# Three edits to a written schedule: weight splits parted from their transposes, the ternary tail spread over the second attention, products of the shared expert put between transposes

## The chip, the core and the metric

The kernel runs on one core of a Trainium2 chip. PE (TensorE) multiplies and transposes, DVE (VectorE), ACT (ScalarE) and POOL (GpSimd) work on rows, SP (SyncE) issues most transfers. The metric is the device time of one execution in microseconds.

## The reference, cut to what matters

Sixteen sequences of 128 rows and 512 columns go through four residual steps, each on a layernormed x:

```python
x = x + tanh(g_xattn[0]) * L0_xattn(layernorm(x), ctx, mask, norm_w, wq, wk, wv, wo, wg)   # 16 heads, gated
x = x + tanh(g_ffn[0])   * L0_ffn(layernorm(x), weight, bias)    # rows quantised to 8 bits, weights to -1, 0, 1
x = x + tanh(g_xattn[1]) * L1_xattn(layernorm(x), ctx, ctx)      # sigmoid(Q'K), 512 x 512 scores
x = x + tanh(g_ffn[1])   * L1_ffn(layernorm(x), ...)             # 16 experts of 352, 4 a token, 2 shared ones
```

In the last step, sigmoid scores over 16 experts pick two of four groups and then four experts for each token; the shared expert (704 hidden columns, in two halves of 352) sees every token.

## The kernel before, in words

Every product of float32 operands is made of three: an operand is split into a high half (a copy rounded by ACT) and a low half (operand less high half, a subtraction on DVE or POOL), and `mm3` multiplies high by high, high by low and low by high. So whatever goes into a product is first transposed by PE into a PSUM bank, copied by ACT, subtracted by DVE.

The first three steps are one block. A list of words, `plan` (line 222 on), is the order of work. Each engine walks the whole plan and does its own part of each word, in order; semaphores with counts derived from the plan hold the engines together. Tiles of 128 rows are numbered 0 to 15; a number in a word is relative to a group of four tiles. The words that matter here:

- `W.k`: weight k is transposed in four tiles (PE) into a ring of four banks, with high halves on ACT and low halves on DVE. The ring (`RING`) is the two score banks, O and REC; a tile waits until the low half of the tile three before it is done.
- `sx` statistics of a tile of x (DVE); `xa`/`ra`, `xb`/`rb`, `xd`/`rd`: the row scales, small sums on DVE with a power on POOL after `ra` and after `rb`; `nm` normalises a tile (DVE); `xT`, `cT` transpose x or the context; `q.0.1`, `k.0.1` are projections of two tiles; `Sa`, `Sb` scores, `sm` softmax, `pT`, `pv`, `bc`, `rc`, `on`, `oT`, `oP` the rest of the heads. `Sa.0` writes the ring's banks and waits until all twenty tiles of weights are split (line 594 on).
- `st`, `ra`, `rb`, `rd`, `u`, `uT`, `fm`, `sf`: the ternary step of a tile: statistics, scales, quantisation on DVE (six instructions), transposes, the product, the sum into x on POOL, statistics for the next step. POOL also adds the bias row at `uT`.
- `an`, `qh`, `ks`: for the second attention, normalisation and high half of q on ACT; `ks` is a copy, a subtraction and the low half of q on POOL. `aS.b.n` are scores of tile b, quarter n, into a bank of the ring; `ag` their sigmoid (twice on ACT, low half on DVE), `aT` transposes the context, `ap` and `aO` the products with it, `aO` also the sum into x and its statistics on DVE. `sw` loads the first half of the shared expert. `ta`, `tb`, `tc` are the row scales for the last step.

The second attention is a loop of 64 steps m (`MS`): step m issues `aS` for m + 3, `ag` for m + 2, then `ap` for m. The dictionary `between` gives the words of the ternary step that come ahead of step m; there, `u.-2` is tile 14, `u.-1` tile 15.

The second block is `routing_and_shared_expert`. Its matrix of normalised rows, XT, is made tile by tile: ACT normalises (`norm`, into one of four places), PE transposes into one of two banks, ACT copies the high half, DVE subtracts the low half, and tile t waits for the low half of tile t - 2. After tiles 5, 9 and 13 PE does the logits of a group of four tiles, a product of the shared expert (`hidden`: eight triples of matmuls, four into bank A for w1 and four into bank B for w3) and the logits by row. `gated` is the silu (ACT), the product (DVE) and its split; it stands on ACT and DVE behind tiles 7, 11 and 15. The shared expert's first half is split in four parts: high halves on ACT (`split_hi`, behind tiles 1, 4 and 5), low halves on POOL. POOL also takes the power for the row scales of the last four tiles, whose sums DVE makes in `row_scale`.

A third block goes through the tiles of the sixteen experts.

Of the kernel before, what the change touches and what calls it, by code (L numbers as in the profile page):

```python
# [18 lines left out]
GB = 4  # L19
# [92 lines left out]
def attention_and_ternary(nc, c, x, g_x, g_f, fw, fb, ctx_in, mask, norm_w, wq, wk, wv, wo, wg, sw1, sw2, sw3):  # L112

    X, identF = c["X"], c["identF"]
    with ExitStack() as st:
# [71 lines left out]
        def steps(text, g):  # L187

            out = []
            for word in text.split():  # L190
# [26 lines left out]
                elif kind in ("xa", "xb", "xd"):  # L217
# [5 lines left out]
        start = ("W.k cT.0 cT.1 W.q sx.0 sx.1 sx.2 sx.3 xa.0 k.0.0 k.0.1 W.v xb.0 k.0.2 k.0.3 xd.0 nm.0 nm.1 W.g xT.0 xT.1 "  # L223
                 "mk.0 mk.1 mk.2 mk.3 q.0.0 q.0.1 nm.2 nm.3 W.o q.0.2 q.0.3 ")
# [3 lines left out]
        for g in range(NG):  # L228
            d = during.get(g, ("",) * 10)
            if g == NG - 1:  # L230
# [20 lines left out]
            "oP.3 uT.0 u.1 aS.0.2 fm.0 uT.1 fm.1 ", NG - 1)  # L251
        between = {0: "sf.-4", 1: "st.-2", 2: "sf.-3", 3: "st.-1", 5: "ra.-1", 6: "rb.-1", 7: "rd.-1 u.-2", 9: "uT.-2", 10: "u.-1",
                   12: "fm.-2", 13: "uT.-1", 16: "fm.-1", 18: "sf.-2", 20: "sf.-1", 22: "ta.1", 24: "tb.1", 26: "tc.1", 28: "sw", 36: "ta.2", 40: "tb.2",
                   42: "tc.2", 52: "ta.3", 56: "tb.3", 58: "tc.3"}
# [78 lines left out]
        with nc.Block() as block:  # L333
# [128 lines left out]
            def _(pe):  # L462
# [55 lines left out]
                for s in plan:  # L518
                    kind, t = s[0], s[1]
                    if kind == "W":  # L520
# [116 lines left out]
            def _(act):  # L637
# [4 lines left out]
                for s in plan:  # L642
                    kind, t = s[0], s[1]
                    if kind == "W":
                        for kc in range(KC):
                            f = KC * ORDER.index(t) + kc
                            act.wait_ge(w_tr, f + 1)
                            act.activation(W[t][:, 0, kc, :], RING[f % len(RING)][:, :], ACT.Copy, scale=scale_of(t, kc))\
                                .then_inc(w_hi, 1)
# [85 lines left out]
            def _(dve):  # L735
# [95 lines left out]
                for s in plan:  # L831
                    kind, t = s[0], s[1]
                    if kind == "W":
                        for kc in range(KC):
                            f = KC * ORDER.index(t) + kc
                            dve.wait_ge(w_hi, f + 1)
                            dve.scalar_tensor_tensor(out=W[t][:, 1, kc, :], in0=RING[f % len(RING)][:, :], scalar=scale_of(t, kc),
                                                     in1=W[t][:, 0, kc, :].bitcast(F32), op0=ALU.mult,
                                                     op1=ALU.subtract).then_inc(w_lo, 1)
# [166 lines left out]
def routing_and_shared_expert(nc, c, m, gate_w, ebias, w1, w2, w3, sw1, sw2, sw3):  # L1006
# [4 lines left out]
    with ExitStack() as st:  # L1011
# [96 lines left out]
        FIRST_SPLIT_AT = (1, 4, 5)  # L1108
# [15 lines left out]
        with nc.Block() as block:  # L1124
# [37 lines left out]
            def _(pool):  # L1162
                for n in range(PARTS):
                    if n == 2:
                        row_power(pool, c, scales, slice(3 * GB, NB), powered)
                    raw, hi, lo = part(0, n)
                    pool.wait_ge(w_hi, n + 1)
                    pool.tensor_tensor(lo, raw, hi.bitcast(F32), ALU.subtract).then_inc(w_lo, 1)
# [50 lines left out]
            def _(pe):  # L1219
# [27 lines left out]
                def hidden(q):  # L1247
# [8 lines left out]
                    for W_, bk in ((W1[b], A[q % 2]), (W3[b], B[q % 2])):  # L1256
                        for k in range(KC):
                            x_ = mm3(pe, bk[0:IC[ch], :], lambda j: W_[:, j, k, cols],
                                     lambda j: XT[:, gr, j, k, :], k == 0, k == KC - 1)
                    x_.then_inc(ab_fill, 1)  # L1260
# [72 lines left out]
                for t in range(NB):  # L1333
# [8 lines left out]
                    if t % GB == 1 and t > GB:  # L1342
                        logit(t // GB - 1)
                        hidden(t // GB - 1)
# [94 lines left out]
            def _(dve):  # L1439
# [221 lines left out]
                def split_lo(n):  # L1661
                    raw, hi, lo = part(1, n)
                    dve.wait_ge(w_hi, PARTS + n + 1)
# [16 lines left out]
                for t in range(NB):  # L1680
# [6 lines left out]
                    if t == GB:  # L1687
# [4 lines left out]
                                      XT[:, t // GB, 0, :, t % GB * P:(t % GB + 1) * P].bitcast(F32), ALU.subtract).then_inc(t_lo, 1)  # L1692
                    if t % GB == GB - 1 and t > GB:
                        gated(t // GB - 1)
# [331 lines left out]
```

## Time and profile before

| what | value |
|---|---|
| three runs, median | 1298.67 us (1297.68 to 1304.92) |
| profiled execution | 1298.22 us |
| its span, first to last instruction | 1296.5 us |
| PE, DVE, ACT, POOL busy | 94%, 52%, 44%, 33% of the span |
| mean granted TensorE clock | 0.981 |

The busy shares are averages over stages with different limits, so the stages have to be read one by one. The granted clock is a share of full speed: 1.00 is 2.4 GHz, 0.50 is 1.2 GHz, and values between are means over a stretch that has both.

### The profile page before, as it was taken

The numbers are of one execution on the slowest core, as the hardware profiler recorded it, in microseconds if no ns is written. First come the engines' busy times: TensorE is split into PE (matmuls) and PEld (weight loads), VectorE is DVE, ScalarE is ACT, GpSimd is POOL, SyncE is SP. The second block draws the span as 40 slices with busy tenths as digits, with TensorE's granted clock in tenths as the row PEclk, the third lists the DMA queues.
The fourth block names the chain that finished last, engine by engine and source line by source line (L and its number), as shares of the span: only waits on it lengthen the run. The fifth ranks groups of instructions, "written<-read, shape, count | busy, mean of one in ns | idle before, by whom it ended". The sixth has DMA issues, their size and how long they took to land. (4 is left out here: it accounts for less than half of the span.)

```text
span 1296.5 us, 25673 instructions
## 1 busy us (share of the span) xinstructions
PE 1215.9 (94%) x7824; PEld 1026.1 (79%) x7836; DVE 668.9 (52%) x1410; ACT 575.7 (44%) x1384; POOL 430.9 (33%) x518
## 2 busy tenths in 40 slices
PE   6998999999999789988999998999999999999995
PEld 6877778788787567666777786889998989999995
DVE  6556545555545799843666644542233553424241
ACT  4555456356356668763121111543334553434342
POOL 1102211210213466340004761244434444343433
PEclk9999999999999889979999999999999999999998
DMA  9100000000000003022000221765446666645554
GB/s 334 36 17 20 18 1 20 18 1 18 17 18 1 26 26 108 8 107 100 1 1 1 91 108 59 249 165 90 76 76 148 176 150 153 146 81 135 86 140 73
DMA packets 54335, 100.36 MB, mean 77 GB/s; under 512 B 5094, under 2 KB 21990, under 8 KB 54262
## 3 DMA queue, kind: packets, MB, share of 16 engines
q0 software_dynamic: 15824, 37.76, 15.5%
q1 hardware_dynamic: 38438, 61.65, 14.7%
q8 instruction: 43, 0.70, 0.2%
q14 instruction: 30, 0.25, 0.1%
HBM read 72.91 MB, written 26.48 MB: 77 GB/s over the span
## 5 line engine op out<-in xcount | busy, mean ns | idle before, releaser
L1876 PE MATMUL t_H<-m_W,t_xT 128*128 128x352 f32 x1632 | 280.2, 327 | 6.4 <-DVE m_W L1954 4.9
L1876 PEld LDWEIGHTS t_H<-m_W,t_xT 128*128 128x128 f32 x1632 | 261.6, 188 | 9.6 <-DVE m_W L1954 7.5
L1844 POOL DMA_INDIRECT out_dram<-t_ys,t_sid x68 | 109.6, 1612 | 220.4 <-ACT t_ys L1905 107.3
L1921 ACT ACTIVATE t_sl<-t_H 128x352 f32<-128x352 f32 x68 | 31.6, 464 | 174.0 <-PE t_H L1876 174.0
L722 ACT ACTIVATE pr<-SC,neg 128x128 f32<-128x128 f32 x256 | 89.9, 377 | 38.2 <-DVE neg L927 38.2
L46 PE MATMUL t_Y<-m_W,t_hT 128*128 128x512 f32 (+1 forms) x207 | 87.4, 422 | 5.2 <-issue 3.1
L1999 DVE TENSOR_TENSOR t_hT<-t_TH,t_hT 128x384 fp32r<-128x384 f32 x68 | 37.8, 556 | 101.9 <-ACT t_hT L1942 100.8
L1905 ACT ACTIVATE t_ys<-t_Y,t_wcol 128x512 f32<-128x512 f32 x69 | 47.4, 687 | 93.7 <-PE t_Y L48 93.7
L1975 DVE TENSOR_TENSOR t_h<-t_H,t_sl 128x352 f32<-128x352 f32 x68 | 35.5, 523 | 102.5 <-ACT t_sl L1921 102.2
L48 PE MATMUL t_Y<-m_W,t_hT 128*128 128x512 f32 (+1 forms) x207 | 81.8, 395 | 0.0
L47 PE MATMUL t_Y<-m_W,t_hT 128*128 128x512 f32 (+1 forms) x207 | 81.5, 393 | 0.0
L451 POOL TENSOR_TENSOR X<-X,upd 128x512 f32<-128x512 f32 x16 | 20.6, 1287 | 139.5 <-DVE upd L908 139.4
L421 POOL TENSOR_TENSOR tmp<-tmp,nhalf 128x2 f32<-128x2 f32 (+2 forms) x22 | 19.6, 892 | 131.6 <-DVE tmp L753 113.0
L667 ACT ACTIVATE pT<-T 128x512 f32<-128x512 f32 x64 | 38.4, 602 | 53.9 <-PE T L488 53.8
L924 DVE TENSOR_REDUCE mx<-SC 128x4 f32<-128x512 f32 x64 | 43.9, 685 | 33.8 <-PE SC L609 33.8
L1197 POOL TENSOR_SCALAR m_W<-m_W,bst 128x128 fp32r<-128x128 f32 x64 | 49.5, 793 | 31.6 <-PE eL L1311 31.4
L853 DVE TENSOR_TENSOR Wq<-kT,Wq 128x512 fp32r<-128x512 f32 x64 | 53.3, 852 | 5.8 <-ACT Wq L713 5.5
L1387 ACT ACTIVATE ehT<-eh 128x512 fp32r<-128x512 f32 (+1 forms) x24 | 15.2, 632 | 91.9 <-DVE eh L1670 91.9
L722 ACT ACTIVATION_READ_ACCUMULATOR pr<-SC,neg 128x1 f32 x256 | 55.3, 216 | 0.0
L1835 POOL COPY t_sid<-m_vals 128x1 uint32 x68 | 49.7, 731 | 0.9 <-issue 0.9
L46 PEld LDWEIGHTS t_Y<-m_W,t_hT 128*128 128x128 f32 (+1 forms) x207 | 39.0, 188 | 13.8 <-issue 5.4
L1950 DVE TENSOR_TENSOR t_xT<-t_TX,t_xT 128x512 fp32r<-128x512 f32 x69 | 47.6, 690 | 3.2 <-ACT t_xT L1898 0.4
(474 smaller groups left out, 3225.6 us busy)
## 6 DMA issues: line engine op xcount, KB each, us to landing
m_raw<-in_L_ffn_w_dram SPq DMA_DIRECT2D x28, 704.0 KB, 5.2
m_raw<-in_L_ffn_w_dram SPq DMA_DIRECT2D x14, 512.0 KB, 6.5
rows_d<-before_w SPq DMA_DIRECT2D x17, 256.0 KB, 2.0
CT<-in_ctx_dram SPq DMA_DIRECT2D x8, 512.0 KB, 3.7
X<-in_x_dram SPq DMA_DIRECT2D x4, 1024.0 KB, 13.9
out_dram<-X SPq DMA_DIRECT2D x3, 1024.0 KB, 4.3
m_raw<-in_L_ffn_w_dram SPq DMA_DIRECT2D x14, 192.0 KB, 6.4
CT<-in_ctx_dram SPq DMA_DIRECT2D x8, 256.0 KB, 2.7
```

Of the source, the lines that this page charges most:

```text
L46: pe.matmul(out, lhs(0), rhs(0), start=first, stop=False)
L47: pe.matmul(out, lhs(0), rhs(1), start=False, stop=False)
L48: return pe.matmul(out, lhs(1), rhs(0), start=False, stop=last)
L722: i = act.activation(pr[:, t % 2, slot, :], SC[t % 2][:, slot * S:(slot + 1) * S], ACT.Exp, scale=SCALE0, bias=neg[:, t % 2, slot:slot + 1 ...
L853: dve.tensor_tensor(as_[:, n, 1, :], asg[:, n, :], as_[:, n, 0, :].bitcast(F32), ALU.subtract).then_inc(as_lo, 1)
L924: dve.tensor_reduce(mx[:, t % 2, :], bk, AX.X, ALU.max).then_inc(s_out, 1)
L1197: i = pool.tensor_scalar(tab_a[t % SLOTS][:, k, :], iP.bitcast(F32), place_p[:, t, k:k + 1], None, ALU.is_equal)
L1835: pool.tensor_copy(sid[:, b:b + 1], m["target"][:, bass.ds(n, 1)]).then_inc(zeroed, 1)
L1844: pool.indirect_dma_start(out=m["out_rows"][:, :], out_offset=bass.IndirectOffsetOnAxis(ap=sid[:, b:b + 1], axis=0), in_=ys[:, b, :], in_o ...
L1876: x_ = pe.matmul(bk[b % 2][:, 0:I], xT[:, b % 2, jx, k, :], W13[:, jw, k, j, :], start=k == 0 and jx == jw, stop=k == KC - 1 and jx == 1)
L1905: act.activation(ys[:, (b - 1) % UT, :], Y[(b - 1) % 2][:, :], ACT.Copy, scale=wcol[:, (b - 1) % UT:(b - 1) % UT + 1]).then_inc(y_evac, 1)
L1950: dve.tensor_tensor(xT[:, b % 2, 1, :, :], TX[:, :].rearrange("p (k t) -> p k t", k=KC), xT[:, b % 2, 0, :, :].bitcast(F32), ALU.subtract) ...
```

## The change

Three things are moved; nothing is computed otherwise.

1. At the beginning a weight's word `W` becomes two for q, v, g and o: `Wt.q`, the transposes on PE, and `Ws.q.0` to `Ws.q.3`, its high and low halves tile by tile on ACT and DVE. The statistics of x come ahead of the splits of q, xT ahead of those of v, and g and o are split between and behind the q products.
2. In the last group of the heads `aT.0` and `aS.0.2` come earlier, and `uT` and `fm` of the group's second tile go into the steps of the second attention. The words of `between` are set at wider distances, up to step 30 instead of 20 for the ternary step.
3. In the routing, `hidden` is done in two halves, w1 behind the transposes of the third tile of a group and w3 behind those of the fourth, and the low halves of the first half of the shared expert go from POOL to DVE, behind tiles 0, 1, 5 and 6.

```diff
-        start = ("W.k cT.0 cT.1 W.q sx.0 sx.1 sx.2 sx.3 xa.0 k.0.0 k.0.1 W.v xb.0 k.0.2 k.0.3 xd.0 nm.0 nm.1 W.g xT.0 xT.1 "
-                 "mk.0 mk.1 mk.2 mk.3 q.0.0 q.0.1 nm.2 nm.3 W.o q.0.2 q.0.3 ")
+        start = ("W.k cT.0 cT.1 Wt.q sx.0 sx.1 sx.2 sx.3 xa.0 Ws.q.0 Ws.q.1 k.0.0 Ws.q.2 k.0.1 xb.0 Ws.q.3 k.0.2 xd.0 nm.0 nm.1 "
+                 "k.0.3 Wt.v xT.0 xT.1 Ws.v.0 Ws.v.1 Ws.v.2 Ws.v.3 q.0.0 Wt.g q.0.1 mk.0 mk.1 mk.2 mk.3 nm.2 nm.3 "
+                 "Ws.g.0 Ws.g.1 Ws.g.2 Ws.g.3 q.0.2 Wt.o q.0.3 Ws.o.0 Ws.o.1 Ws.o.2 Ws.o.3 ")
...
-            "oP.2 rb.0 pv.6 pT.14 rc.3 aS.0.0 pT.15 rd.0 bc.3 aT.0 pv.7 on.3 oT.3 u.0 aS.0.1 ag.0.0 aT.1 ag.0.1 "
-            "oP.3 uT.0 u.1 aS.0.2 fm.0 uT.1 fm.1 ", NG - 1)
-        between = {0: "sf.-4", 1: "st.-2", 2: "sf.-3", 3: "st.-1", 5: "ra.-1", 6: "rb.-1", 7: "rd.-1 u.-2", 9: "uT.-2", 10: "u.-1",
-                   12: "fm.-2", 13: "uT.-1", 16: "fm.-1", 18: "sf.-2", 20: "sf.-1", 22: "ta.1", 24: "tb.1", 26: "tc.1", 28: "sw", 36: "ta.2", 40: "tb.2",
-                   42: "tc.2", 52: "ta.3", 56: "tb.3", 58: "tc.3"}
+            "oP.2 rb.0 pv.6 pT.14 rc.3 aS.0.0 pT.15 aT.0 rd.0 bc.3 pv.7 on.3 oT.3 u.0 aS.0.1 ag.0.0 aT.1 aS.0.2 ag.0.1 "
+            "oP.3 uT.0 u.1 fm.0 ", NG - 1)
+        between = {2: "uT.-3", 3: "sf.-4", 4: "fm.-3 st.-2", 6: "st.-1", 8: "ra.-1 sf.-3", 10: "rb.-1", 12: "rd.-1 u.-2", 17: "uT.-2",
+                   18: "u.-1", 20: "fm.-2", 23: "uT.-1", 25: "sf.-2", 26: "fm.-1", 28: "sw", 30: "sf.-1", 32: "ta.1", 34: "tb.1", 36: "tc.1",
+                   44: "ta.2", 48: "tb.2", 50: "tc.2", 52: "ta.3", 56: "tb.3", 58: "tc.3"}
...
-                    if kind == "W":
-                        for kc in range(KC):
+                    if kind in ("W", "Ws"):
+                        for kc in s[2:] or range(KC):
...
-        FIRST_SPLIT_AT = (1, 4, 5)
+        FIRST_SPLIT_AT, FIRST_LOW_AT = (1, 4, 5), (0, 1, 5, 6)
...
-                for n in range(PARTS):
-                    if n == 2:
-                        row_power(pool, c, scales, slice(3 * GB, NB), powered)
-                    raw, hi, lo = part(0, n)
-                    pool.wait_ge(w_hi, n + 1)
-                    pool.tensor_tensor(lo, raw, hi.bitcast(F32), ALU.subtract).then_inc(w_lo, 1)
+                row_power(pool, c, scales, slice(3 * GB, NB), powered)
...
-                    for W_, bk in ((W1[b], A[q % 2]), (W3[b], B[q % 2])):
+                    for W_, bk in [((W1[b], A[q % 2]), (W3[b], B[q % 2]))[n] for n in halves]:
...
-                    x_.then_inc(ab_fill, 1)
+                    if 1 in halves:
+                        x_.then_inc(ab_fill, 1)
...
                     if t % GB == 1 and t > GB:
                         logit(t // GB - 1)
-                        hidden(t // GB - 1)
+                    if t % GB == 2 and t > GB:
+                        hidden(t // GB - 1, (0,))
+                    if t % GB == 3 and t > GB:
+                        hidden(t // GB - 1, (1,))
                         logit_rows(t // GB - 1)
...
+                    if t in FIRST_LOW_AT:
+                        split_lo(FIRST_LOW_AT.index(t), 0)
```

## Rows read from the trace of the kernel before

**Rows 1.** The page, the line of busy engines.

```profile
PE 1215.9 (94%) x7824; PEld 1026.1 (79%) x7836; DVE 668.9 (52%) x1410; ACT 575.7 (44%) x1384; POOL 430.9 (33%) x518
```

**Rows 2.** Windows by stage: length, engines busy, clock, DMA share, GB/s.

```profile
0.00:39.24 39.24, 27.45 (x195) 26.44 (x197) 22.43 (x50) 18.45 (x35) 3.79 (x15) 0.96 0.80 285
39.24:421.00 381.76, 365.92 (x3269) 299.03 (x3279) 208.41 (x529) 198.45 (x729) 73.64 (x64) 1.00 0.06 15
421.00:549.00 128.00, 114.61 (x539) 86.75 (x539) 110.43 (x188) 95.64 (x181) 70.73 (x58) 0.95 0.14 42
549.00:609.15 60.15, 49.28 (x230) 35.35 (x230) 21.69 (x38) 29.90 (x46) 13.06 (x15) 0.86 0.31 111
609.15:807.55 198.40, 191.75 (x862) 149.63 (x862) 118.62 (x262) 34.10 (x52) 66.23 (x90) 0.99 0.12 41
807.55:1296.50 488.95, 466.93 (x2733) 428.91 (x2733) 187.28 (x344) 199.17 (x342) 203.48 (x277) 0.99 0.58 129
```

**Rows 3.** Timeline of PE: start, us, instruction, count, idle before it.

```profile
29.48 0.55 PE L46 MATMUL M<-xT,Wq 128*128 128x256 f32 x1 [3.20 <-DVE xT L872]
...
33.91 0.38 PE L474 MATMUL SC<-identF,pr 128*128 128x128 f32 x2
...
35.58 0.37 PE L46 MATMUL M<-xT,Wq 128*128 128x256 f32 x1
...
38.40 0.28 PE L48 MATMUL M<-xT,Wq 128*128 128x256 f32 x1
39.24 0.39 PE L601 MATMUL SC<-mrow,onesB 1*128 1x512 bf16 x2 [0.56 <-ACT qT L689]
```

**Rows 4.** Timeline of DVE at the start.

```profile
16.64 2.46 DVE L879 BATCH_NORM_STATS2 bst<-X 128x6 f32<-128x512 f32 x4
...
35.27 1.41 DVE L837 SCALAR_TENSOR_TENSOR Wo<-SC,hg,Wo 128x512 fp32r<-128x512 f32 x2 [4.48 <-ACT Wo L648]
...
37.26 0.74 DVE L837 SCALAR_TENSOR_TENSOR Wo<-REC,hg,Wo 128x512 fp32r<-128x512 f32 x1
```

**Rows 5.** Windows in four stretches, for the granted clock.

```profile
30.00:31.00 1.00, 1.00 (x7) 1.00 (x6) 0.79 (x2) 0.00 (x0) 0.00 (x0) 0.50 1.07 395
...
438.00:440.00 2.00, 2.00 (x7) 1.35 (x5) 1.06 (x2) 0.46 (x1) 0.66 (x2) 0.50 0.00 0
...
459.00:461.00 2.00, 2.00 (x6) 1.61 (x5) 2.00 (x4) 1.91 (x4) 0.24 (x1) 0.50 0.01 4
...
600.00:605.00 5.00, 5.00 (x17) 3.28 (x16) 0.69 (x1) 2.16 (x3) 0.00 (x0) 0.71 0.07 21
```

**Rows 6.** Who PE waited for, 421 to 549 us: total, times, longest.

```profile
PE T L488 <- DVE fu L803: 6.0, 2, 3.8
PE M L46 <- DVE oT L941: 1.6, 1, 1.6
PE SC L46 <- POOL Wk L444: 1.4, 2, 0.8
PE REC L631 <- DVE rec L933: 1.0, 1, 1.0
PE M L500 <- ACT fuT L672: 0.9, 1, 0.9
```

**Rows 7.** POOL's groups from 421 to 549 us: count, busy us, mean ns.

```profile
L444 POOL TENSOR_TENSOR Wk<-xn,Wk 128x512 fp32r<-128x512 f32 x14 | 20.2, 1441 | 31.1 <-ACT Wk L705 31.1
```

**Rows 8.** Who PE waited for, 549 to 609 us.

```profile
PE eY L1338 <- DVE XT L1691: 6.8, 6, 2.9
...
PE eL L1236 <- DVE XT L1691: 1.6, 1, 1.6
```

**Rows 9.** Timelines of DVE and of POOL at the beginning of the routing.

```profile
552.29 3.16 DVE L91 TENSOR_TENSOR mean<-bst 128x4 f32<-128x4 f32 x1
...
552.27 3.16 POOL L1168 TENSOR_TENSOR m_W<-shared_raw,m_W 128x1408 fp32r<-128x1408 f32 x1 [11.18 <-ACT m_W L1373]
```

**Rows 10.** Line 1664, the second half's low halves on DVE: ns min/median/max.

```profile
L1664 DVE TENSOR_TENSOR eW<-m_raw,eW x4: 683/1416/1618, 660.7 to 717.7; 128x1408 fp32r<-128x1408 f32 x2, 128x1024 fp32r<-128x1024 f32 x1, 96x512 fp32r<-96x512 f32 x1
```

More of the change, by code:

```diff
@@ L519, in _ @@
                     kind, t = s[0], s[1]
-                    if kind == "W":
+                    if kind in ("W", "Wt"):
                         weight(t)
@@ L643, in _ @@
                     kind, t = s[0], s[1]
-                    if kind == "W":
-                        for kc in range(KC):
+                    if kind in ("W", "Ws"):
+                        for kc in s[2:] or range(KC):
                             f = KC * ORDER.index(t) + kc
@@ L832, in _ @@
                     kind, t = s[0], s[1]
-                    if kind == "W":
-                        for kc in range(KC):
+                    if kind in ("W", "Ws"):
+                        for kc in s[2:] or range(KC):
                             f = KC * ORDER.index(t) + kc
@@ L1245, in logit_rows, with hidden @@
                     i.then_inc(logits, 1)
-                def hidden(q):
+                def hidden(q, halves=(0, 1)):
                     u, ch = q // 3, q % 3
@@ L1659, in tile_rows, with split_lo @@
                         .then_inc(meta_ok, 1)
-                def split_lo(n):
-                    raw, hi, lo = part(1, n)
-                    dve.wait_ge(w_hi, PARTS + n + 1)
+                def split_lo(n, b=1):
+                    raw, hi, lo = part(b, n)
+                    dve.wait_ge(w_hi, PARTS * b + n + 1)
                     dve.tensor_tensor(lo, raw, hi.bitcast(F32), ALU.subtract).then_inc(w_lo, 1)
```

## The prediction

> **What bounds the kernel now.** I read the page first: PE is busy for 94% of the span [rows 1], so a change can only pay where PE waits or where its clock is low. The windows by stage [rows 2] show where that is. From 39.24 to 421 us, and from 609 us on, PE is busy for some 96% of the time at a granted clock of 0.99 to 1.00; those stages are chains of products, and a shift ahead of them is carried to the end. The three stages that the change touches are the loose ones: the start (27.45 busy of 39.24 us), the end of the heads with the second attention (114.61 of 128.00 us, clock 0.95), and the routing (49.28 of 60.15 us, clock 0.86). Then I read, stage by stage, who PE waited for [rows 3, 6, 8], and the queues of DVE, ACT and POOL in order of time. ACT, DVE and POOL work through the same written plan as PE, in order, so moving a word in the plan moves it past everything queued on each of them.
>
> **Part one, the start.** What it removes: DVE's low halves of Wv and Wg stood between the statistics of x and the low half of xT, and the first q product waited 3.20 us for that [rows 3, 4]. From the first statistics (16.64) to q.0.0 (29.48) it took 12.84 us. Four low halves take 2.73 us (35.27 to 38.00, [rows 4]). Eight of them leave this stretch and the four of Wq enter it: 2.7 less. The two POOL powers between are then covered by less DVE work; I charge 0.9 as an estimate, which leaves 1.8. The statistics may also begin up to 2.7 earlier, as Wq's low halves no longer precede them, if x has landed. No row shows when it landed, so the gain lies between 1.8 and 4.5; I take the middle, 3.1.
>
> What it adds: the transposes are parted from the splits. Wt.g comes to stand between q.0.0 and q.0.1, while W.g filled a time in which PE had to wait for x anyway: 1.7 more (four tiles from 33.91 to 35.58, [rows 3]). On ACT, Ws.g now stands behind the eviction of q.0.1, and Wt.o needs the four banks that Ws.g frees. The chain from first transpose to last low half of a weight took 4.1 us (33.91 to 38.00, [rows 3, 4]); without the first tile's transposes (0.4) and with an eviction ahead (0.56, [rows 3]) it is 4.25. Wt.o thus ends some 4.8 after q.0.1, and q.0.3 1.55 later: 6.35, where it was 4.77 (33.91 to 38.68): 1.6 more. Last, Sa.0 waits for all twenty low halves, and Ws.o now stands behind q.0.3 on ACT: Sa.0 follows q.0.3 by 4.25 where it followed by 0.56: 3.7 more. So 7.0 lost against 3.1 won: 3.9 later.
>
> The gap before Sa.0 also touches the clock. After the 3.20 us gap the clock was at 0.50, 1.2 GHz [rows 5], and q.0.0 with q.0.1 took 4.43 us where q.0.2 with q.0.3 took 3.10 [rows 3]: 1.3 lost. The new gap is longer, so I add 1.3 (bounds 0 and 1.3), and leave the old fall before q.0.0 in place, since PE is mostly idle there in the new order too; without it 1.3 would come back. **The start: 5.2 us later** (bounds 1.2 and 6.5). The Trainium skill has the same reading (TensorE: Matmul & The Clock Gate, "What's actually happening"): the low clock is the resting state and activity lifts it, so an order that trades one gap for another keeps paying; the row at 30 us agrees.
>
> **Part two, the tail.** Before, the last heads ended with u.13, uT.13 and fm.13 in a row, and tile 14 followed within the first steps. PE waited 6.0 us for two quantisations, 1.6 for oT, 1.0 for rec, 0.9 for uT, and 1.4 for POOL's low half of q [rows 6]: 10.9. After the gaps the clock lay at 0.50 twice, some 6 us each [rows 5]; PE was busy for about 10.6 us of that, half of which is lost: 5.3. So 16.2 can be won. I worked the new order forward by the durations of the old one. aT.0 goes into the wait for rec (0.55 of it is left), aS.0.2 into that for oT (0.5 left). With aS.0.2 gone from its old place, fm.0 waits about 1.3 for ACT's uT. uT.13 finds its tile ready. What is late next: ap.1.0 waits 0.4 for DVE to empty aO.0's bank. POOL has fm.12's and uT.13's adds before ks.2, so aS.2.0 waits 1.1. At step 12, ks.4 stands on POOL behind the second power, which waits for DVE's rb; casts, subtraction and aq's low half (1.44 a row, [rows 7]) then end 1.8 to 2.7 after PE wants aS.4.0: 2.2. And u.15 on DVE holds back the eviction of aO.4: 1.7. Sum of the new waits 7.75. The clock fell behind the gaps of 3.20 and 3.8 us and not behind that of 1.6; a fall cost 2.7 here (half of 5.3), and for the gap of 2.2, between these rows, I take half of one, 1.3 (bounds 0 and 2.7). **The tail: 16.2 - 7.75 - 1.3 = 7.2 us earlier** (bounds 3 and 11, as POOL keeps pace with PE or not). The adds and statistics moved to steps 8 to 30 lie beside products; without that cover each add is 1.3.
>
> **Part three, the routing.** PE waited 6.8 us before transposes and 1.6 before the last logits for the low half of XT [rows 8]. With two banks and one pair of copies a tile, ACT and DVE pace four transposes in a row while the product of 5.6 us stands in one piece. Between transposes, each half covers a tile. In the steady part the waits were 1.06 and 0.56 in two groups and 1.57 at the end: 4.8, all of it covered. The stretch of the last logits ran at a clock of 0.71 after that wait [rows 5]: 29% of 5 us, 1.4, comes back. At the beginning DVE's first small sum took 3.16 us, begun 0.02 us after POOL's 3.16 us low half [rows 9]; its six sisters take 0.15 to 0.17. That block of 3.0 goes with POOL's work, but DVE now does two low halves of the 1408 columns, 1.4 to 1.6 each [rows 10], ahead of XT's third low half. Net 0.8 won. What queues behind the new waits: ACT's gated(q) now waits for a half product that PE issues after tile 7's transposes, and tile 8's copy stands behind it; by the rows it is ready just as PE comes to tile 10. **The routing: 7.0 us earlier** (bounds 3.5 and 8). The Trainium skill (SBUF - State Buffer, "Who interferes with whom") says that a DVE instruction with two SBUF inputs and a GpSimd instruction that reads SBUF exclude each other for the whole instruction. Rows 9 agree; by that rule the moved low halves still shut POOL out, but its one power there is 1.0 us, so the sum stays.
>
> **Sum.** The profiled execution took 1298.22 us (span 1296.5 and 1.7 around it), 0.45 below the median of 1298.67. 1298.2 + 5.2 - 7.2 - 7.0 = 1289.2.
>
> **Rivals.** First: the start gains what its gap promised. The 3.1 us at q.0.0 would be carried on, if Ws.o were done by the time of q.0.3; then 1298.2 - 3.1 - 7.2 - 7.0 = 1280.9. For it speaks that ACT was idle 5 us before q.0.0's eviction; against it that Ws.o stands behind q.0.3 in the plan. Second: the second attention takes its gain back. POOL, with 1.44 us for a low half [rows 7] and the adds spread over seven tiles, becomes the pace: the 7.2 are lost, 1296.4. The Trainium skill's rule of exclusion is the mechanism behind such a pace; rows 9 show one case. Third: ACT, waiting for half products, starves the transposes in the routing: half of part three is lost, 1292.6. Fourth, slower: the new waits on POOL, one in each tile, keep the clock at 1.2 GHz through steps 8 to 26 of the second attention. At that clock three products took 1.28 us where they otherwise take 0.69, so a tile of eight such triples and its transposes costs some 5.1 us more. 1.8 tiles eat the sum, from 3.1 tiles on the kernel is slower by more than 0.5%; all 4.5 tiles give 1312. Against it: after both falls the clock came back within 7 us though waits went on.
>
> **How the numbers follow.** The forecast has 0.57 (1284 to 1294), the first rival 0.10, the second 0.15, the third 0.14, the fourth 0.04. Under 0.5%, 6.5 us, a measurement of this kernel can't be told from no change; 1292.2 is the border. The forecast's own range lies four fifths under it (0.46), with the first rival and half of the third 0.63 faster; 0.33 the same; 0.04 slower. The range 1281 to 1297 holds the forecast and the second and third rivals, 0.86.
>
> **What would show it.** Right: q.0.0 begins near 26.4, but Sa.0 only near 43 to 44; a gap of some 4 us before Sa.0; no gap over 2.5 us between 421 and 475; aS.4.0 waits for POOL; DVE L91 takes 0.15; no wait for XT before tiles 8, 9, 12, 13. Wrong: Sa.0 at or before 39.24, a low clock through more than one tile after 450, or gaps before transposes in the routing.

## The result, and the profile after

The changed kernel takes 1295.38 us (median of 13 executions, 1291.82 to 1299.50); the kernel before took 1304.35 beside it (13 executions, 1297.68 to 1306.27). The ratio is 0.9942, with a 95% interval of 0.9927 to 0.9958: faster by 0.58% (0.42 to 0.73), where the prediction had set 0.5% as the least that can be told from no change. Of the 13 executions of the kernel before, five took 1297.68 to 1299.51 us and eight 1303.31 to 1306.27; the profiled one (1298.22), on which the forecast was built, is like the five. The changed kernel's profiled execution took 1294.01 us (span 1292.3), 4.2 less. The forecast was 1289.2, so the time is 6 us above it: outside the forecast's own 1284 to 1294, inside the wide range of 1281 to 1297. The forecast's three terms were +5.2 (start), -7.2 (tail) and -7.0 (routing); I read them off one by one.

The page's line of busy engines, for [rows 1], and the windows by stage, for [rows 2] (length, then busy time of PE, PEld, DVE, ACT, POOL, then clock, DMA share, GB/s):

```profile
PE 1212.3 (94%) x7823; PEld 1023.5 (79%) x7836; DVE 672.5 (52%) x1414; ACT 575.9 (45%) x1384; POOL 424.8 (33%) x514
```

```profile
0.00:40.82 40.82, 26.25 (x196) 24.32 (x198) 22.67 (x50) 17.80 (x35) 3.80 (x15) 0.98 0.77 274
40.82:425.84 385.02, 368.48 (x3269) 300.44 (x3279) 208.66 (x529) 198.80 (x729) 73.77 (x64) 0.99 0.05 15
425.84:552.05 126.21, 112.41 (x538) 85.20 (x539) 111.28 (x188) 95.85 (x181) 72.08 (x58) 0.97 0.14 43
552.05:603.80 51.75, 45.96 (x230) 34.03 (x230) 23.58 (x42) 30.03 (x46) 5.02 (x11) 0.90 0.37 130
603.80:801.68 197.88, 191.39 (x862) 149.50 (x862) 118.70 (x262) 34.13 (x52) 66.42 (x90) 0.99 0.12 41
801.68:1292.30 490.62, 467.85 (x2733) 430.00 (x2733) 187.56 (x344) 199.32 (x342) 203.75 (x277) 0.99 0.57 129
```

The busy shares are those of before, so as totals they say nothing. By stage: the beginning is 1.58 us longer, the heads 3.3 longer (with the same work), the second attention 1.8 shorter, the routing 8.4 shorter. In the second attention PE's idle time did not fall: 128.00 less 114.61 before, 126.21 less 112.41 after, which is 13.39 and 13.80 us. What it won there is 2.2 us of busy time, at a clock of 0.97 in place of 0.95. PE's timeline at the start answers [rows 3]; under it stand four windows, one at q.0.0 and three around Sa.0:

```profile
26.06 0.36 PE L46 MATMUL M<-xT,Wq 128*128 128x256 f32 x1 [1.65 <-DVE xT L873]
...
32.83 0.41 PE L475 MATMUL SC<-identF,pr 128*128 128x128 f32 x2 [0.51 <-DVE Wg L838]
...
40.82 0.61 PE L602 MATMUL SC<-mrow,onesB 1*128 1x512 bf16 x2 [3.97 <-issue]
```

```profile
26.00:28.00 2.00, 1.94 (x16) 1.97 (x17) 2.00 (x4) 1.27 (x4) 0.00 (x0) 1.00 1.05 386
...
38.00:40.00 2.00, 0.00 (x0) 0.00 (x0) 2.00 (x4) 1.58 (x3) 0.00 (x0) 0.80 0.00 0
...
42.00:44.00 2.00, 2.00 (x14) 1.47 (x12) 0.01 (x1) 0.60 (x1) 0.00 (x0) 0.50 0.00 0
...
46.00:48.00 2.00, 2.00 (x7) 1.52 (x6) 0.24 (x2) 2.00 (x13) 0.00 (x0) 0.50 0.05 12
```

q.0.0 begins 3.4 us earlier than before, and Sa.0 1.58 later: the gap ahead of Sa.0 is there as forecast (3.97 us), reached sooner than forecast. At q.0.0, behind a gap of 1.65 us, the clock is at 1.00, where it was at 0.50 before. But from the gap ahead of Sa.0 to 48 us the clock is at 0.50, with PE busy all the time from 42 us on. The transposes of cT.2 begin at 49.57; before, they began at 44.14: 5.43 late, of which 3.85 arose behind Sa.0.

PE's waits from the last heads to the end of the second attention answer [rows 6], those of the routing [rows 8], DVE's first small sum [rows 9]:

```profile
PE SC L46 <- POOL Wk L445: 5.4, 5, 2.2
PE M L46 <- DVE X L859: 2.7, 1, 2.7
PE M L46 <- issue: 2.1, 2, 1.1
PE M L501 <- DVE upd L909: 1.1, 1, 1.1
...
PE REC L632 <- DVE rec L934: 0.6, 1, 0.6
PE M L46 <- DVE oT L942: 0.5, 1, 0.5
```

```profile
PE eY L1335 <- DVE before_w L1676: 2.5, 1, 2.5
PE eY L1335 <- ACT before_w L1394: 1.7, 1, 1.7
PE eY L1335 <- DVE XT L1691: 1.7, 2, 1.0
```

```profile
555.34 0.15 DVE L91 TENSOR_TENSOR mean<-bst 128x4 f32<-128x4 f32 x1
```

The two waits of 6.0 us in all for a quantisation are gone, and so are 6.7 us of waits for XT. What PE waits for in the second attention is now above all POOL (5.4 us) and one sum of DVE's (2.7).

The table takes the same instructions in each trace: the time in the kernel before, and by how many us a kernel is later (+) or earlier (-). The four lower lines are the first four experiments.

| | Sa.0 | Sa.2 | aS.0.0 | routing's first transposes | experts' first transposes | PE's last |
|---|---|---|---|---|---|---|
| before, us | 39.24 | 58.06 | 419.72 | 551.43 | 807.55 | 1285.72 |
| changed | +1.58 | +5.44 | +4.84 | +3.05 | -5.87 | -4.11 |
| beginning alone | +2.29 | +5.37 | +5.27 | +4.93 | +8.99 | +9.43 |
| tail alone | +0.74 | +0.75 | +1.01 | -0.63 | +1.10 | +2.21 |
| routing alone | +1.95 | +1.96 | +1.15 | -0.30 | -9.01 | -5.90 |
| tail and routing | +0.94 | +0.96 | +0.36 | -1.37 | -10.00 | -6.99 |

In the changed kernel the beginning costs 4.8, the tail wins 1.8 (4.84 to 3.05), the routing 8.9, and 1.8 of that is given back among the experts, so that 7.2 are left at the end. The term that failed is the tail's.

### The profile page after: what moved, and what is told of

Same layout as the page of the kernel before. It is cut to its first block and busy times, and to the rows that moved or that the text cites. A ratio compares the mean times of both kernels' runs of the same rounds, so it can differ in the third digit from the quotient of the medians.

```text
span 1292.3 us, 25672 instructions
## 1 busy us (share of the span) xinstructions
PE 1212.3 (94%) x7823; PEld 1023.5 (79%) x7836; DVE 672.5 (52%) x1414; ACT 575.9 (45%) x1384; POOL 424.8 (33%) x514
## 5 line engine op out<-in xcount | busy, mean ns | idle before, releaser
L854 DVE TENSOR_TENSOR Wq<-kT,Wq 128x512 fp32r<-128x512 f32 x64 | 53.3, 855 | 5.4 <-ACT Wq L714 5.2
```

The costliest lines, as they stand in the source:

```text
L854: dve.tensor_tensor(as_[:, n, 1, :], asg[:, n, :], as_[:, n, 0, :].bitcast(F32), ALU.subtract).then_inc(as_lo, 1)
```

## The experiments

### One part at a time

The beginning alone:

```diff
 # kernel before, with
-start = ("W.k cT.0 cT.1 W.q sx.0 ...")
+start = ("W.k cT.0 cT.1 Wt.q sx.0 ... Ws.o.0 Ws.o.1 Ws.o.2 Ws.o.3 ")
```

> The kernel before with the new order of the beginning alone. By the offsets of the two traces the beginning costs about 4.8 us, whatever follows it: Sa.0 near 40.8 us with a gap of about 4 us ahead of it, clock 0.50 from there to about 48 us, routing and second attention as before, span 1301 to 1302. The rival, that the later stages absorb a late beginning (their first waits are for loads and other engines, which a shift leaves where they are), would give a span within 2 us of 1296.5.

1307.28 us (median of 10) beside 1301.81 for the kernel before; ratio 1.0033 (1.0011 to 1.0055). Sa.0 had the same 3.97 us ahead of it, and of the 5.3 us at aS.0.0 4.9 were left at the routing: next to nothing absorbs a late beginning. The 4 us more at the experts' first transposes arose in the routing, together with the delay that the next experiment shows.

The tail alone:

```diff
 # kernel before, with
-"... rd.0 bc.3 aT.0 pv.7 ...", between = {0: "sf.-4", ...}
+"... aT.0 rd.0 bc.3 pv.7 ...", between = {2: "uT.-3", ...}
```

> The kernel before with the new end of the heads and the new steps of the second attention alone. If what this edit brings is limited by its own queues (POOL's low half of q, DVE's sum into x ahead of tile 5), it gives about 1.8 us here too: span near 1294.7, with PE waiting 2 to 2.7 us ahead of aS.4.0 and of ap.5.0 again. The rival, that the edit is worth the 7.2 us of the sum and lost the rest only in company with the late beginning, gives a span near 1289.3 and neither of these waits.

1299.12 us (10 executions), ratio 0.9967 (0.9950 to 0.9984). From aS.0.0 to the routing it wins 1.64 (+1.01 to -0.63), with the same waits as in the changed kernel. So the tail's small gain is its own and no consequence of the late beginning. It is nearer 0.9 than 1.8: in the four profiled executions with the old tail and no other change to that stage it takes 130.26 to 131.71 us (mean 131.0, the profile of before being the longest), in five with the new tail 129.92 to 130.94 (mean 130.2).

The trace shows something else as well: this execution lost 2.9 us at the first logits, in code that is that of before. Timelines of POOL and of DVE there:

```profile
555.32 3.15 POOL L1168 TENSOR_TENSOR m_W<-shared_raw,m_W 128x1408 fp32r<-128x1408 f32 x1 [0.52 <-ACT m_W L1373]
```

```profile
555.47 3.03 DVE L97 TENSOR_SCALAR tmp<-tmp 128x4 f32<-128x4 f32 x1
```

A DVE instruction on 4 columns takes 3.03 us, begun 0.15 us after a subtraction of POOL, and ends with it; in the profile of before the same instruction took 0.17, just ahead of POOL's second subtraction. With the beginning alone it took 3.07. This is [rows 9] a second time, and here it is a matter of chance: the code is the same in all three kernels.

The routing alone:

```diff
 # kernel before, with
+FIRST_LOW_AT = (0, 1, 5, 6)     # POOL's low halves to DVE
-    hidden(t // GB - 1)
+    hidden(t // GB - 1, (0,)) at the third tile, (1,) at the fourth
```

> The kernel before with the routing's edit alone. If the halves of the product between the transposes are what takes the waits away, it gives about 7.2 us alone: span near 1289.3, waits for XT under 2 us, clock 1.00 from 565 to 610 us. The rival, that part of the gain came from the stage being reached at another time against its loads, gives a gain of 5 us or less.

1292.47 us (4 executions, 1291.96 to 1293.06), ratio 0.9912 (0.9880 to 0.9944). The stage wins 8.7 us, and its waits for XT are 1.7. At the end 5.6 of the 8.7 are left; the rest goes among the experts, whose stage I did not take apart.

Tail and routing, with the old beginning:

```diff
 # changed kernel, with
-start = ("W.k cT.0 cT.1 Wt.q ...")
+start = ("W.k cT.0 cT.1 W.q ...")
```

> The changed kernel with the old order of the beginning. If the three parts add up, it takes the gain of the tail and of the routing without the cost of the beginning: span near 1287.5 (9 us under before, 4.8 under the changed kernel). If the parts hang together, the sum of the other three runs does not give this one; a span of 1290 or more would say so.

1290.87 us (4 executions), ratio 0.9894 (0.9859 to 0.9928), span 1289.7. Faster than the changed kernel, as the sum says, though 2 us short of the span expected: it reaches Sa.0 0.9 later than before did (the three kernels of this group with the old beginning, 0.7 to 2.0), and gives back 3 us among the experts. Part of the late Sa.0 is the clock: behind the same gap of 3.20 us ahead of q.0.0 it stayed at 0.50 for 3.4 us in the profile of before, and for 6.8 us here and with the routing alone.

The low halves of the shared expert on DVE, with the product in one piece:

```diff
 # the routing alone, with
-    hidden(t // GB - 1, (0,)) at the third tile, (1,) at the fourth
+    hidden(t // GB - 1) at the second tile, as before
```

> The kernel before, with one half of the routing's edit: the low halves of the first half of the shared expert go to DVE, and the product stays in one piece. If what changes from one execution of the kernel before to the next is whether DVE's last small sum is caught behind POOL's second low half (0.17 us in the profiled one, 3.03 and 3.07 in two profiled runs that keep the old routing), both blocks of 3 us go: the first logits begin 1.3 us earlier than in the profile of before, the times lie within 2 us of each other, and their median is 1296 to 1298, 4 to 5 us under that of before. The rival, that the steady waits ahead of tiles 8, 9, 12 and 13 hold all of the gain, leaves times spread from 1298 to 1306 with the median of before. Both leave those four waits (1.06 and 0.56 us twice) in place.

1297.18 us, four executions within 1.4 us (1296.01 to 1297.36), beside 1303.40; ratio 0.9948 (0.9932 to 0.9965). DVE L91 took 0.14 and L97 0.17, and the first logits came 1.43 earlier against the stage's beginning. The waits for XT stayed (5.6 and 1.6). So this half takes away the chance delay, and the product's halves take away the steady waits: 8.7 less the 0.5 that this kernel wins in the stage against the profiled execution of before. Whether the delay is all that spreads the times of the kernel before is not shown: with it the stretch from the routing's first transposes to the experts' took 1.7 us (tail alone) and 4.1 us (beginning alone) longer than in the profile of before, while the 13 times of that kernel range over 8.6 us; and the changed kernel, in whose profile DVE's small sums are not delayed, still ranges over 7.7.

### The gap ahead of Sa.0

A product put into the gap:

```diff
-"... q.0.3 Ws.o.0 Ws.o.1 Ws.o.2 Ws.o.3 "     ... "sm.1 v.0 st.-2 ..." in group 0
+"... q.0.3 Ws.o.0 Ws.o.1 Ws.o.2 Ws.o.3 v.0 " ... "sm.1 st.-2 ..." in group 0
```

> The changed kernel, with the product v.0 of the first group taken from behind the first scores and put between q.0.3 and Sa.0, where PE waited 3.97 us for the last low half of Wo. It is 2.8 us of products, so the wait should shrink to 1.1 to 1.3 us. If the low clock from 40.8 to 48 us is what the gap ahead of it leaves behind, it goes too: the transposes of cT.2 then begin near 43 us (49.57 in the changed kernel), and the kernel is 6 to 6.7 us faster. The rival, that the clock falls because of how little PE did from 27 to 41 us altogether, gives the 2.8 us alone, with 0.50 still shown behind Sa.0. A third: the softmax of the first heads now has 2.8 us less beside it, and PE waits before pT.0 for what it won.

1291.96 us, ratio 0.9907 (0.9891 to 0.9924). PE's timeline:

```profile
41.00 0.39 PE L603 MATMUL SC<-mrow,onesB 1*128 1x512 bf16 x2 [1.19 <-issue]
...
42.99 0.66 PE L490 MATMUL T<-identF,CT 128*128 128x128 f32 x4
...
48.82 0.63 PE L490 MATMUL T<-identF,pr 128*128 128x128 f32 x4 [1.54 <-ACT xT L666]
```

```profile
38.00:41.00 3.00, 1.81 (x9) 1.17 (x7) 2.94 (x5) 1.76 (x4) 0.00 (x0) 1.00 0.00 0
41.00:44.00 3.00, 2.77 (x27) 2.14 (x28) 1.36 (x3) 0.60 (x1) 0.00 (x0) 1.00 0.00 0
44.00:48.00 4.00, 3.28 (x16) 2.42 (x15) 1.31 (x4) 3.39 (x18) 0.00 (x0) 1.00 0.02 6
```

The low clock is gone altogether and cT.2's transposes begin at 42.99 instead of 49.57: the fall followed the gap, and what PE did before 36 us is the same in both kernels. (The product also adds to PE's work from 27 to 41 us, so the second case is made unlikely and not ruled out.) At Sa.2 4.2 us are won, 4.4 against q.0.0; of the 2.4 that this lacks against cT.2's 6.6 the third case took 1.54, ahead of pT.0.

The high halves of Wo ahead of q.0.3:

```diff
-"... q.0.2 Wt.o q.0.3 Ws.o.0 Ws.o.1 Ws.o.2 Ws.o.3 "
+"... q.0.2 Wt.o Ws.o.0 Ws.o.1 Ws.o.2 Ws.o.3 q.0.3 "
```

> The changed kernel, with the high halves of Wo ahead of q.0.3 in the plan instead of behind it. If Sa.0 came late only because ACT and DVE took up Wo behind the eviction of q.0.3 (its transposes were done 1.5 us earlier), ACT makes the high halves from about 33.5 us on, the last low half is done near 37.5, Sa.0 begins near 37.7 (40.82 in the changed kernel), no low clock follows, and the kernel is some 7 us faster (3.1 of the wait, 3.85 of the clock). The rival, that DVE, which makes the masks and normalises two tiles in this stretch, sets the time of the low halves, leaves Sa.0 near 40; then no more than 1 us is won, and the clock falls as before.

1289.78 us (4 executions, 1288.68 to 1290.39), ratio 0.9900 (0.9872 to 0.9928): the lowest median of the study, if by 0.6 us only. DVE's last low half of Wo, and PE's Sa.0:

```profile
36.61 0.74 DVE L838 SCALAR_TENSOR_TENSOR Wo<-REC,hg,Wo 128x512 fp32r<-128x512 f32 x1
```

```profile
37.57 0.39 PE L602 MATMUL SC<-mrow,onesB 1*128 1x512 bf16 x2 [0.66 <-ACT qT L690]
```

Sa.0 is 3.25 us earlier than in the changed kernel, Sa.2 7.12, aS.0.0 6.26. One word in the wrong place turned a beginning that wins (1.4 us at aS.0.0) into one that loses.

### The tail

The product fm of tile 14 one step earlier:

```diff
-18: "u.-1", 20: "fm.-2", 23
+18: "u.-1", 19: "fm.-2", 23
```

> The changed kernel with one word moved by one step: the product fm of tile 14 from step 20 to step 19. Products of fm and sums of the second attention share two banks, and at step 20 the single fm between aO.4 and aO.5 gives ap.5.0 the bank that DVE has not yet emptied of aO.4, because u.15 stands before it on DVE. If that is why PE waited 2.67 us there, the wait goes (0 to 0.5 us comes up ahead of ap.4.0), the clock of 0.71 from 480 to 485 us goes too, and by the next steps some 3.5 us are won, of which the wait for POOL ahead of aS.8.0 (1.5) can take a part: 2 to 3.5 us faster in the end. The rival, that DVE as a whole is behind, moves the wait to the next product: within 0.7 us of the changed kernel.

1299.85 us, 4.5 us slower than the changed kernel by the trace at the routing. The wait at ap.5.0 went (2.67 to 0.42), and a wait of 4.64 for POOL came ahead of aS.6.0: POOL's sum now stands ahead of ks.6 and waits for DVE, which is at u.15. POOL's and PE's timelines:

```profile
479.10 1.65 POOL L460 TENSOR_TENSOR X<-X,upd 128x512 f32<-128x512 f32 x1 [6.29 <-DVE upd L916]
```

```profile
479.12 0.47 PE L46 MATMUL M<-Wq,Wv 128*128 128x512 f32 x1 [0.42 <-DVE upd L916]
484.69 0.79 PE L46 MATMUL SC<-Wk 128*128 128x512 f32 x1 [4.64 <-POOL Wk L445]
```

The second power behind ks.4:

```diff
-10: "rb.-1", 12: "rd.-1 u.-2", 17
+12: "rb.-1", 14: "rd.-1 u.-2", 17
```

> The changed kernel with the second small sum and power of tiles 14 and 15 behind ks.4 instead of ahead of it (rb from step 10 to 12, rd and u.14 from step 12 to 14). If POOL came late with the low half of q for tile 4 because it waited for DVE's sums ahead of the second power, the wait of 2.25 us ahead of aS.4.0 falls under 0.6 us and the 0.74 of clock behind it goes: 2 to 3.5 us faster at tile 5, if u.14, now 2 steps later, is not waited for. The rival, that POOL's own work paces this stretch (adds and low halves of 1.2 to 1.8 us each), leaves a wait of 1.5 us or more at aS.4.0 or moves it to aS.5.0.

1294.99 us, and 0.1 us of difference from the changed kernel between aS.0.0 and the routing. The wait at aS.4.0 went, as the first theory had it, and came back as 4.23 us for DVE, where u.14 now stood:

```profile
471.96 0.77 PE L46 MATMUL M<-Wq,Wv 128*128 128x512 f32 x1 [4.23 <-DVE Wv L866]
```

```profile
465.84 1.61 DVE L797 TENSOR_SCALAR fu<-X,mean,rstd 128x512 f32<-128x512 f32 x1
...
468.78 1.31 DVE L804 TENSOR_SCALAR fu<-fu,fsc 128x512 f32<-128x512 f32 x1
```

The words set wider still:

```diff
-between = {2: "uT.-3", 3: "sf.-4", 4: "fm.-3 st.-2", ... 12: "rd.-1 u.-2", ... 20: "fm.-2", ... 26: "fm.-1", ... 30: "sf.-1", ...
+between = {2: "uT.-3", 3: "sf.-4", 5: "fm.-3", ... 17: "u.-2", ... 24: "fm.-2", ... 30: "fm.-1", ... 33: "sf.-1", ...
```

> The changed kernel with the ternary words of the second attention spread further still: fm.13 at step 5, the sums and powers at 12 to 16, u.14 at 17, its product at 24, u.15 at 22, its product at 30, the last statistics at 33. If the stretch fails by its density (DVE and POOL each have too much in steps 4 to 26), the waits shrink and 2 to 4 us are won. If each lone fm costs a wait of its own through the bank that it takes, or the total of DVE's work sets the length, the result lies within 1 us of the changed kernel.

1294.57 us; 0.7 us won between aS.0.0 and the routing, no more than that stage differs between executions. The sums of waits are of the same size (4.6 for DVE ahead of two ap, 4.3 for POOL): density by itself is not the cause.

Less work on DVE, and less on POOL:

```diff
+w_ = slice(0, 8 if t >= NB - GB else D)
-dve.tensor_scalar(u[:, :], X[:, t, :], ...)      # and the reduction, and the rounding
+dve.tensor_scalar(u[:, w_], X[:, t, w_], ...)
```

> The changed kernel; the quantisation of tiles 12 to 15 is done on 8 of its 512 columns (the other columns are left out), which takes about 8 us from DVE between 425 and 490 us and nothing from POOL. DVE was busy for 63 of the 70 us from 430 to 500, more than PE. If DVE's load is what the spread words run into, the stage from aS.0.0 to the first transposes of the routing (129.9 us) gets 5 to 8 us shorter, and the waits for DVE's sum ahead of ap.5.0 (2.7) go, with part of those for POOL, whose inputs come from ACT and DVE. If POOL's queue is what paces it, the stage shortens by less than 1.5 us and the 5.1 us of waits for POOL stay.

```diff
+w_ = slice(0, 8 if t >= NB - GB else D)
-pool.tensor_tensor(X[:, t, :], X[:, t, :], brow[:, :], ALU.add)     # and the sum with upd
+pool.tensor_tensor(X[:, t, w_], X[:, t, w_], brow[:, w_], ALU.add)
```

> The changed kernel; POOL's sums into x of the ternary step (bias row and product) for tiles 12 to 15 are done on 8 of 512 columns (the rest is left out), which takes 8 additions of 1.3 to 1.7 us, some 10 us, from POOL and nothing from DVE's own work. If POOL's queue paces the stretch, its 5.1 us of waits go and the stage gets 5 us shorter or more. If DVE's load does, the waits ahead of ap.5.0 stay and the stage gains 2 us or less, out of instructions of DVE that no longer run beside an addition.

The first kernel quantises only 8 of the 512 columns of tiles 12 to 15, the second adds only 8 columns of the bias row and of the product; the rest is left out. The stage from aS.0.0 to the routing (129.92 us in the changed kernel) takes 127.79 with less on DVE and 124.25 with less on POOL: 2.1 and 5.7 won. (Their total times, 1317.98 and 1313.99, are not to be compared: other values of x lead to other routes, and the experts take 24 us longer.) From 430 to 500 us DVE was busy for 62.58 us with less on DVE, and for 63.19 in the changed kernel: hardly less, though 1.7 us of it are two instructions that only now fall into the stretch. The groups of DVE's instructions in that stretch, with less on DVE first, the changed kernel second:

```profile
L855 DVE TENSOR_TENSOR Wq<-kT,Wq 128x512 fp32r<-128x512 f32 x33 | 32.8, 1014 | 2.9 <-ACT Wq L714 2.9
...
L798 DVE TENSOR_SCALAR fu<-X,mean,rstd 128x8 f32<-128x8 f32 x4 | 3.0, 755 | 0.0
```

```profile
L854 DVE TENSOR_TENSOR Wq<-kT,Wq 128x512 fp32r<-128x512 f32 x32 | 29.4, 939 | 2.8 <-ACT Wq L714 2.7
...
L866 DVE TENSOR_TENSOR Wv<-T,Wv 128x512 fp32r<-128x512 f32 x7 | 4.8, 685 | 1.6 <-ACT Wv L660 1.6
...
L797 DVE TENSOR_SCALAR fu<-X,mean,rstd 128x512 f32<-128x512 f32 x4 | 4.1, 1013 | 0.0
```

And one of the four, with what POOL does beside it (timelines of DVE and POOL, less on DVE):

```profile
462.13 1.19 DVE L798 TENSOR_SCALAR fu<-X,mean,rstd 128x8 f32<-128x8 f32 x1
```

```profile
462.03 1.26 POOL L445 TENSOR_TENSOR Wk<-xn,Wk 128x512 fp32r<-128x512 f32 x1
```

With 8 columns instead of 512 the instruction takes 755 ns in place of 1013; in the heads, where POOL does little, all 512 columns take 541. Two of the four took 0.29 us; the other two took 1.19 and 1.26 us, begun beside an instruction of POOL's that was under way, and ended with it. The three groups of the quantisation together went from 10.5 to 5.5 us, not to the 2.5 expected, and the subtraction of two operands in SBUF (L854) got longer, 939 to 1014 ns. L866, which reads one operand from PSUM, takes 685 ns throughout. With less on POOL nothing was taken from DVE, and yet its subtraction took 824 ns in place of 939 (less on POOL):

```profile
L856 DVE TENSOR_TENSOR Wq<-kT,Wq 128x512 fp32r<-128x512 f32 x35 | 28.3, 824 | 4.7 <-ACT Wq L716 4.7
```

So part of DVE's time in this stretch is POOL's.

The casts of tiles 2 to 8 on ACT, on top of the early Wo; and the same with the wider words:

```diff
 # ACT, behind qh, for tiles 2 to 8 (left out on POOL):
+act.activation(ak[:, t % 2, 0, :], aCX[t % GB], ACT.Copy).then_inc(ak_hi, 1)
```

> The changed kernel with the high halves of Wo ahead of q.0.3, and with the casts of the context for tiles 2 to 8 (seven of POOL's instructions, 0.6 to 1.15 us each, 6 to 7 us in all) done by ACT behind the high half of q; no work is left out. If the time that POOL's instructions take is what the spread words run into, the waits for POOL ahead of aS.2.0, aS.3.0, aS.4.0 and aS.8.0 (5.4 us in all) go down by at least half, and the stage is 2.5 to 3.5 us shorter than the 129.98 us it takes in the kernel with Wo alone moved: a time near 1287. If only the additions count, because they hold back DVE (two operands in SBUF on both engines) where a cast does not, the stage gains less than 1 us. A third: ACT, busy for 50 of 70 us there, comes late with the high half of q and of the sigmoids, and nothing is won.

> As the kernel with the casts on ACT, with the ternary words set at the wider distances as well. By itself the wider setting gave 0.1 to 0.7 us. If POOL's time and the density of the words are two causes that hide each other, both together win more than their sum: a stage of 125 us or less. If not, it lies within 1 us of the kernel with the casts alone.

1295.06 and 1298.42 us. The stage got 5.7 and 9.6 us longer than with Wo alone moved. In 70 us POOL was busy for 32.20 instead of 44.03, DVE for 58.71 instead of 63.82, and yet PE's waits for POOL doubled (casts on ACT):

```profile
PE SC L46 <- POOL Wk L447: 10.5, 6, 2.4
```

POOL's subtraction now waits for ACT's cast, which stands behind ACT's sigmoids. The third case comes nearest, and the two theories fall in this form: what PE waits for here is a chain from ACT's high half over POOL to the scores.

That chain begun two steps earlier, on ACT alone and on both engines:

```diff
+if n == 1 and b + 2 < NB:
+    text += [f"qh.{b + 2}"]              # second kernel: f"qh.{b + 2} ks.{b + 2}"
 if n == KC - 1 and b + 2 < NB:
-    text += [f"qh.{b + 2} ks.{b + 2}"]
+    text += [f"ks.{b + 2}"]              # second kernel: left out
```

> The changed kernel with the high halves of Wo ahead of q.0.3, and with ACT's high half of q (qh) two steps earlier in the second attention, at the second step of each tile instead of the fourth; POOL's word ks stays where it is. With the casts on ACT, POOL was busy for 32 instead of 44 of 70 us and PE waited 10.5 us for it instead of 5.4, so what PE waits for looks like the chain from ACT's high half to POOL's low half, begun too late. If so, PE's waits for POOL fall from 5.4 to 3 us or less and the stage of 129.98 us gets 2 to 4 us shorter. The rival, POOL's own queue, keeps them at 4 us or more, and the stage stays within 1 us.

> As the kernel with qh alone earlier, with POOL's ks two steps earlier as well, so that POOL's three instructions for a tile begin 3 us sooner, ahead of the additions and powers of the ternary step that stand at those steps. If the start of the chain is all there is to it, both kernels win the same. If POOL's queue and the chain both count, this one wins more: waits for POOL under 1.5 us, no low clock after 460 us, the stage 5 us shorter, a time near 1285. If what is won there only moves to DVE (its sum ahead of ap.5.0, 2.7), the gain stays under 2 us.

1291.35 and 1290.39 us, stages 1.8 and 1.6 us longer than with Wo alone moved. ACT alone leaves 4.6 us of waits for POOL. With both moved, PE's waits are:

```profile
PE M L46 <- DVE Wq L854: 4.1, 2, 2.7
PE M L46 <- issue: 2.5, 2, 1.7
PE M L46 <- DVE Wv L866: 2.4, 2, 2.1
PE M L46 <- DVE X L859: 2.0, 1, 2.0
PE SC L46 <- POOL Wk L445: 1.1, 1, 1.1
```

POOL is waited for by 1.1 us only, DVE, in three lines, for 8.5.

## Why the prediction was right or wrong

**The tail, -7.2, measured -1.8: the step that failed.** The old waits went as the prediction said, and each new wait was there: fm.0 1.1 (1.3 forecast, for ACT; it was for DVE), rec 0.6, oT 0.5, aS.2.0 0.7 (1.1), aS.4.0 2.25 (2.2), ap.5.0 2.67 (1.7). Missing from the sum were 0.6 at aS.3.0, 1.07 ahead of ap.1.0 (0.4 forecast), 1.03 ahead of ap.6.0 and 1.5 at aS.8.0. With 7.75 of new waits for 10.9 of old ones PE's idle time should have fallen by 3.2 us; it rose by 0.4. So 3.6 of the 5.4 us that were not won are waits. The other 1.8 are the clock: 4.0 us of it were to come back (5.3 less 1.3), and 2.2 did, since it fell twice where half a fall was counted:

```profile
460.00:465.00 5.00, 2.75 (x8) 1.93 (x7) 4.75 (x10) 2.39 (x5) 4.53 (x4) 0.74 0.00 0
...
480.00:485.00 5.00, 5.00 (x19) 3.98 (x19) 4.37 (x5) 1.49 (x3) 4.05 (x3) 0.71 0.01 3
```

The prediction misread its own trace here. It named gaps of 3.20 and 3.8 us as those behind which the clock fell, and one of 1.6 behind which it did not. But the first fall of the old tail came behind 2.27 us, as PE's timeline before shows, and that of the last logits behind 1.57 [rows 5, 8]:

```profile
435.34 0.81 PE L488 MATMUL T<-identF,fu 128*128 128x128 f32 x4 [2.27 <-DVE fu L803]
```

So a gap of 2.2 us could bring a whole fall, and one of 1.7 could not be taken as harmless.

On the waits, the working let a wait vanish when its word was moved. The runs show waits that move on to the next word: DVE was busy for 63 of 70 us in this stretch, its time is partly POOL's, and of the seven kernels that only moved words or work there, none won more than 0.7 us. Leaving out work did: 2.1 on DVE, 5.7 on POOL. The second rival, that POOL becomes the pace and the gain is lost, had the right place and, with the whole 7.2 lost where 5.4 were, nearly the right price; it was given 0.15. Its mechanism is half shown at best, since taking casts off POOL made things worse. The Trainium skill (SBUF - State Buffer, "Who interferes with whom") says that DVE and GpSimd (POOL) share one pair of ports, which `tensor_scalar` can take as well as instructions with two operands in SBUF, and that the one that comes second is blocked for the whole of the first. The 8 columns at 1.19 us and the 3.03 us of L97 agree. Longer instructions are not what the sum lacked, though: over the second attention DVE was busy for 110.43 us before and 111.28 after, POOL for 70.73 and 72.08, so the old durations already held this. What stays open is how the 5.7 us divide between POOL's queue and DVE's blocked instructions: no run parted them.

**The start, +5.2, measured +4.8: right in sum by two errors.** The wins and losses on PE's own path came out 1.58 instead of 3.9. Some 0.3 us of that is x coming sooner (3.4 won at q.0.0, forecast 3.1); most of the rest is the clock, which did not fall ahead of q.0.0. The prediction had left that fall in place and said that 1.3 would come back without it. This was luck in part: in three of the 13 profiled executions with this order up to q.0.0, behind the same 1.65 us, it did fall there, and Sa.0 came 1.6 us later. The fall behind the new gap cost 3.85 instead of 1.3, and 3.0 to 3.1 in the six other profiled executions with that gap. It was sized by [rows 3, 5], where the products behind the gap took 1.3 longer; here the 0.50 lasted to 48 us although PE was busy. The mechanism, Ws.o behind q.0.3, was right; undoing it alone is worth 6.3 us at aS.0.0. So the first rival (Wo done by the time of q.0.3) named the cure. Its time, 1280.9, needed the tail's 7.2 too.

**The routing, -7.0, measured -8.9 in its stage and -7.2 at the end.** The steady waits went, the halves paying for most of it, as forecast. Not foreseen were that the chance delay of 3 us at L97 is also removed, which the profiled execution of before did not have, and that 1.8 us are given back among the experts. The profiled executions differ by 4.2 us and the medians by 9.0; that the forecast, too, lay 9.0 under its starting point is luck, since its terms were worked out from the profiled execution. The third rival left a trace, one wait of 0.97 us ahead of tile 10: DVE's low half of tile 8 stood behind the gated product, for which ACT waited for the second half product. (The 1.7 us of waits for ACT's rows lie ahead of tile 4, before the first half product.) It did not take half.

**The fourth rival**, a low clock through several tiles, did not come: there were two falls, each over within 4 us.

## What to carry to other kernels

When a word is parted from another, check each engine's queue for what the later half now stands behind: here one word's place was worth 6 us. Where two engines hold each other back, waits on them move rather than vanish, so count both engines' work in the stretch together before crediting a removed wait. And profile several executions before sizing a change: 3 us here hung on which of two instructions came first, and behind one and the same gap the clock stayed low for 3.4 us in one execution and 6.8 in another.

## What the runs showed of the hardware

A fall of the clock can outlast the gap by much: behind 3.97 us without work, PE stayed at 0.50 (1.2 GHz) to 48 us, about 7 us, while windows of 2 us show it busy throughout from 42 us on. It can also come after the gap: in the six other profiled executions with this gap the clock fell only as PE began again or up to 1 us later, and stayed at 0.50 for 6.8 us with PE busy all the while. Two windows of the kernel with the second power behind ks.4, where Sa.0 begins at 42.60:

```profile
42.60:43.50 0.90, 0.90 (x11) 0.77 (x12) 0.00 (x0) 0.00 (x0) 0.00 (x0) 1.00 0.00 0
43.75:50.25 6.50, 6.50 (x22) 4.92 (x21) 2.22 (x5) 3.52 (x17) 0.00 (x0) 0.50 0.01 4
```

The length of one gap does not decide it: in the kernel before the clock fell behind 1.57 us (last logits) and not behind 1.65 (the wait for oT, [rows 6]); behind gaps of 1.19 and 1.54 us in the kernel with the filled gap it stayed at 1.00.

And a DVE instruction on 4 or 8 columns can take as long as POOL's instruction beside it: 3.03 us in place of 0.17, 1.19 where another on 8 columns took 0.23.
